# A macaron block on one NeuronCore: the last attention batch moved into the third expert pass, its scatters paced one per pair, and the projection's bias added by GpSimd

## The chip, the cores and the metric

One Trainium2 chip, one of its NeuronCores. The metric is the device time of the whole program in microseconds. Before: median 693.09 us of 3 runs (692.06 to 694.55).

## The reference

x is 16 x 256 x 128 (4096 tokens of 128 channels). Three residual steps, each on the layer-normalised rows:

```python
x = x + 0.5 * moe(layernorm(x))     # 16 experts, top 2
x = x + attention(layernorm(x))     # 16 heads of 8, causal, 256 keys
x = x + 0.5 * moe(layernorm(x))

def moe(xt):
    logits = xt @ Wg.T + bg;  top_vals, top_idx = top_k(logits, 2);  rw = softmax(top_vals)
    gate, up = even, odd columns of xt @ Wgu[e] + bgu[e]
    gated = (clip(up, -7, 7) + 1) * gate * sigmoid(1.702 * gate)     # gate <= 7
    out = sum over the two experts of rw * (gated @ Wd[e] + bd[e])
def attention(x):
    q, k, v = split(x @ W_attn + b_attn);  y = softmax(causal(q k^T / sqrt(8))) v
    return y @ W_proj + b_proj
```

## The kernel before

**Tiles and passes.** The tokens are 32 tiles of 128 rows, in 8 quads of 4 tiles, in 2 sides of 4 quads. Each of the two expert stages routes its tokens: VectorE normalises a quad (`normalise`), TensorE turns it (`transposes`, line 1651) and multiplies by the router's weights (`logits`, 1659), VectorE finds the top two (`top2`), TensorE counts ranks (`ranks`), VectorE makes row numbers (`positions`), and GpSimd scatters each tile's rows twice into `rows_by_expert` in HBM by indirect DMA (`scatter`, line 595; j counts 8 scatters to a quad). A side's rows are then read back, sorted by expert, in 47 tiles, that is 24 pairs. There are four expert passes: 0 and 1 for the first stage, 2 and 3 for the second, one for each side. In the second stage GpSimd gathers the results of pass 2 while pass 3 runs, and those of pass 3 after it (line 530), and VectorE adds them up.

**An expert pass** is a pipeline of slots of one pair, written out by `expert_passes` for each engine. In slot s TensorE turns pair s-1 (`turn_x`, 1740), makes gate and up of pair s-2 (`gate_up`, 1752) and the down product of pair s-4 (`down`, 1764); ScalarE copies xT, takes the sigmoid (866), copies the next weights (854) and issues the store (873); VectorE does `gate` (1292, 1293, 1295; called gate 0, 1, ... by pair) and `evac_y` (1309). SP loads the tiles a turn of eight ahead, in its queue's order: pass 3's loads stand behind all of pass 2's, a table and `s_scat[1]`. After its steps each engine calls a hook, `last_groups` in pass 2, with the slot's number `at`: it holds the routing of the last quads, 6 (`MERGED`) and 7. `s_y` counts finished pairs.

**The attention** between passes 1 and 2 is 64 units of 4 heads of one batch, 4 to a batch, 16 batches, written out in `unit` for each engine; `Steps` says which further steps stand in a unit. TensorE makes scores two units ahead (`late_scores` 1396, `early_scores` 1403), turns the row maxima (1419), makes the transposed scores with mask and maxima (`weights`, 1435 to 1459), and multiplies by the values (`weigh_values`, 1518); ScalarE takes the exponential (715) and copies maxima (709); VectorE takes the row maxima (921, 938). A batch ends with `tokens_first` (1526), `divide`, `channels_first` (1532), `project_out` and `add_attention` (952), which stand in the units of the next batch; for the last batch they stand after all units. `project_out` begins with a product of 3 rows of ones by the bias in three BF16 parts (1537) and adds eight products of the projection (1541) to it in bank 7. The parts are made once by `split_biases` in the first routing and spread by three DMAs of SP. GpSimd's work in the attention (low parts of q and k, adds of expert results at line 553, gathers, scatters of quads 0 to 5) waits for units by `a_max` and `a_pv`. The w_tile buffer of the expert passes lies over pT, the exponentials.

Of the kernel before, what the change touches and what calls it, by code (L numbers as in the profile page):

```python
# [20 lines left out]
ALU = mybir.AluOpType  # L21
# [116 lines left out]
def build_block(nc, x, w_g, g_last, w_gu, up_last, w_d, b_d, attn_last, b_proj, w_attn, w_proj, konst, out):  # L138
    ctx = ExitStack()
    with ctx:  # L140
# [29 lines left out]
        bias_in = sb("bias_in", [1, C])  # L170
        bias_hi = sb("bias_hi", [1, C], BF16)
        bias_mid = sb("bias_mid", [1, C], BF16)
        bias_lo = sb("bias_lo", [1, C], BF16)
        bias3 = sb("bias3", [3, C], BF16)
# [137 lines left out]
        s_bias3 = sem("s_bias3")  # L312
# [115 lines left out]
        def _(sp):  # L428
# [6 lines left out]
            sp.dma_start(bias_in[:, :], b_proj).then_inc(s_bias3, 16)  # L435
# [12 lines left out]

            sp.wait_ge(s_setup, 3)
            for r, part in enumerate((bias_hi, bias_mid, bias_lo)):  # L450
                sp.dma_start(bias3[r:r + 1, :], part[:, :]).then_inc(s_bias3, 16)
# [58 lines left out]
        def _(pool):  # L510
# [38 lines left out]
            def add_result(x, k):  # L549

                mine = xr[:, x * QUAD:(x + 1) * QUAD, :]
                pool.wait_ge(a_half, 2 * x + 1 + k)
                nc.gpsimd.tensor_tensor(mine, mine, yg_of_token[:, :, k, :], ALU.add).then_inc((a_half, a_comb)[k], 1)

# [47 lines left out]
            for f in range(2):  # L602
                if f == 0:
# [31 lines left out]
                    for x in range(1, B // 2):  # L635
# [24 lines left out]
                        if later:  # L660
                            root_of_pair(x + 1)
                        if latest:
# [8 lines left out]
                        else:  # L671
# [4 lines left out]
                            scatter(1, range(26, 37), in_units(u, u, u, u + 1, u + 1, u + 2, u + 2, u + 2, u + 3, u + 3, u + 4))  # L676
                            root(1, MERGED, *GROUPS_2[MERGED])
                            scatter(1, range(37, 48), in_units(u + 5, u + 5) + [(a_pv, u + n) for n in (5, 5, 6, 6, 6, 7, 7, 7, 8)])
                else:
                    root(1, NQ - 1, *GROUPS_2[NQ - 1])  # L680
                    scatter(1, of_quads(6, 8))
# [7 lines left out]
        def attention_scalar(act, normalise_rows, router):  # L689
# [53 lines left out]
            def unit(t, s):  # L743
                t, s = t + s // UNITS, s % UNITS
                steps = Steps(t, s)
                normalise_part(steps, t, s, 0)
                if steps.max_next:
                    evac_max(*after(t, s, 1))
# [9 lines left out]
                exp(t, s)  # L758
# [20 lines left out]
            def units():  # L779
                evac_max(0, 0)  # L780
                attention_units(unit)
                evac_sums(B - 1)
                evac_y_channels(B - 1)

            return first_pair, units

        @block.scalar
        def _(act):
# [28 lines left out]
            for f in range(2):  # L817
                if f == 0:
                    first_pair, units = attention_scalar(act, normalise_rows, router)
# [7 lines left out]
                def last_groups(p, t, k):  # L827
                    if p == SIDES:
                        at = t * DUOS + k
                        if at == 0:  # L830
                            evac_xn(1, MERGED)
                        if at == 4:
# [12 lines left out]
                def copy_weights(p, t, k):  # L845
                    if isinstance(t, int) and (t, k) == (0, 0):
                        act.wait_ge(s_tab, 32 * (p + 1))
                    key = (p, t if isinstance(t, int) else str(t), k // 2)
# [30 lines left out]
        def attention_vector(dve, ch, router, in_tiles):  # L879
# [69 lines left out]
            def add_attention(b):  # L949
                dve.wait_ge(a_proj, b + 2)  # L950
                rows = xs[:, bass.ds((b + 1) * QT, QT), :].rearrange("p n c -> p (n c)")
# [51 lines left out]
            def units():  # L1003
# [4 lines left out]
                divide(B - 1)  # L1008
                add_attention(B - 1)

            return first_pair, units

        @block.vector
        def _(dve):
# [10 lines left out]
            for f in range(2):  # L1025
# [99 lines left out]
                def split_biases():  # L1125
                    dve.wait_ge(s_bias3, 16)
                    ch.mark(nc.vector.tensor_copy(bias_hi[:, :], bias_in[:, :]))
                    ch.wait()
                    ch.mark(nc.vector.tensor_tensor(bias_in[:, :], bias_in[:, :], bias_hi[:, :], ALU.subtract))
                    ch.wait()  # L1130
                    ch.mark(nc.vector.tensor_copy(bias_mid[:, :], bias_in[:, :]))
                    ch.wait()
                    ch.mark(nc.vector.tensor_tensor(bias_in[:, :], bias_in[:, :], bias_mid[:, :], ALU.subtract))
                    ch.wait()
                    nc.vector.tensor_copy(bias_lo[:, :], bias_in[:, :]).then_inc(s_setup, 1)

# [103 lines left out]
                if f == 0:  # L1240
                    first_pair, units = attention_vector(dve, ch, router, in_tiles)
# [694 lines left out]
```

## Time and profile before

| | |
|---|---|
| median of 3 runs | 693.09 us |
| the profiled execution | 689.52 us |
| its span | 687.7 us |
| TensorE, VectorE, ScalarE, GpSimd busy | 70%, 70%, 47%, 50% of the span |
| first routing | to about 78 us |
| passes 0 and 1 | 78 to 196 us, with the first attention steps |
| attention | 200 to 507 us |
| passes 2 and 3 | 511 to 633 us |
| last gathers and adds | to the end |

How to read it: the profile is of one execution. A row of an order of time gives start, duration (both us), engine, line, operation, output <- input and, in brackets, how long the engine stood idle before and what ended that. "PE" is TensorE's products, "DVE" VectorE, "ACT" ScalarE, "POOL" GpSimd. "issue" is a wait that the profile doesn't explain; "remote" one whose releaser it can't name. An engine of which nobody waits costs nothing by being idle.

### The profile page before, as it was taken

What the parts mean: (1) busy time and instruction counts of PE and PEld (TensorE: products, weight loads), DVE (VectorE), ACT (ScalarE), POOL (GpSimd) and SP (SyncE); (2) the same over time, 40 slices, a digit from 0 to 9 for tenths busy, and PEclk for the clock granted to TensorE, in tenths of its full rate; (3) what the DMA queues carried; (4) which work ended last, traced back from release to release, by engine and by line L of the source; (5) the groups of instructions that cost most, each with busy time, mean ns of one, the idle gap of its engine ahead of it and who ended that gap; (6) DMA issues with size and microseconds to landing.
All of it is one profiled execution on the core that took longest, in us unless ns stands there. A gap on an engine that the chain in (4) does not pass through costs nothing.

```text
span 687.7 us, 18833 instructions
## 1 busy us (share of the span) xinstructions
PE 483.6 (70%) x6375; PEld 340.5 (50%) x6375; DVE 482.4 (70%) x2459; ACT 326.6 (47%) x646; POOL 342.4 (50%) x355
## 2 busy tenths in 40 slices
PE   2443488897848898988888888776866789876000
PEld 2433366775625565655555555544445568665000
DVE  6778476887757787889898977766436498666612
ACT  1001376776505656665656564543434378664000
POOL 3757555446356464545454554444524400456774
PEclk9999999998859999999999988999658789999555
DMA  9931255555565362626262523502012335544432
GB/s 268 357 123 47 84 150 155 150 155 136 168 185 181 101 210 70 216 64 215 64 202 75 189 95 126 163 32 63 32 33 85 93 108 152 142 139 127 118 84 62
DMA packets 106294, 89.72 MB, mean 130 GB/s; under 512 B 10977, under 2 KB 98530, under 8 KB 105826
## 3 DMA queue, kind: packets, MB, share of 16 engines
q1 hardware_dynamic: 72130, 59.51, 28.0%
q0 software_dynamic: 8192, 16.79, 8.3%
q10 hardware_dynamic: 25888, 12.34, 6.1%
q8 instruction: 47, 0.77, 0.5%
q14 instruction: 37, 0.30, 0.1%
HBM read 46.93 MB, written 41.68 MB: 129 GB/s over the span
## 4 chain that ended last, share of the span: by engine, by line
PE 44%; DVE 18%; issue 14%; ACT 6%; another core or an unknown queue 6%; POOL 5%; DMA 4%; ACTq 2%; DVEq 0%; SPq 0%; POOLq 0%
PE banks L1752 9%; POOL by_token L530 5%; PE banks L1518 4%; DVE by_token L921 4%; PE banks L1459 3%; PE banks L1403 3%; PE banks L1764 3%; PE banks L1740 2%; PE banks L1659 2%; PE banks L1435 2%; PE banks L1444 2%; PE banks L1439 2%; PE banks L1368 1%; PE banks L1541 1%
## 5 line engine op out<-in xcount | busy, mean ns | idle before, releaser
L921 DVE CUSTOM_DVE_ANT_0 by_token<-banks,konst_sb 128x256 f32<-128x256 f32 (+1 forms) x512 | 151.0, 353 | 41.1 <-PE banks L1403 28.4
L595 POOL DMA_INDIRECT rows_by_expert<-by_token,posi x120 | 118.1, 984 | 109.2 <-DVE maxima L938 39.2
L715 ACT ACTIVATE pT<-banks 128x1536 f32<-128x1536 f32 x64 | 92.9, 1451 | 79.9 <-PE banks L1459 76.8
L1752 PE MATMUL banks<-xT,pT 128*64 128x128 f32 x1504 | 112.1, 289 | 24.8 <-ACT xT L861 10.9
L1752 PEld LDWEIGHTS banks<-xT,pT 128*64 128x64 f32 x1504 | 86.5, 143 | 45.9 <-issue 30.0
L530 POOL DMA_INDIRECT yg<-results_by_tile,tilepos x64 | 62.0, 969 | 77.8 <-DVE maxima L938 38.5
L530 POOL DMA_INDIRECT by_token<-results_by_tile,tilepos x64 | 62.1, 970 | 69.1 <-DMA results_by_tile<-ysb 41.4
L854 ACT ACTIVATE pT<-w_experts 128x384 f32 x188 | 88.2, 516 | 17.5 <-remote 5.5
L1292 DVE SCALAR_TENSOR_TENSOR sig<-banks,sig 128x256 f32<-128x256 f32 x96 | 39.8, 414 | 45.5 <-ACT sig L866 34.0
L1764 PE MATMUL banks<-pT,gT 128*64 128x128 f32 x752 | 62.8, 282 | 3.4 <-DVE ysb L1309 1.6
L866 ACT ACTIVATE sig<-banks 128x256 f32<-128x256 f32 x96 | 36.2, 377 | 51.3 <-PE banks L1752 26.0
L1444 PE MATMUL banks<-q_stack,k_stack 64*128 64x256 bf16 x256 | 58.8, 279 | 0.0
L1518 PE MATMUL banks<-pT,by_token 128*32 128x256 f32 (+1 forms) x1024 | 58.1, 347 | 0.0
L1309 DVE TENSOR_TENSOR ysb<-banks,w_experts 128x128 f32<-128x128 f32 x188 | 45.7, 283 | 15.0 <-PE banks L1764 7.0
L1435 PE MATMUL banks<-mT,select 64*128 64x256 bf16 x256 | 48.6, 279 | 3.3 <-ACT pT L715 3.1
L1764 PEld LDWEIGHTS banks<-pT,gT 128*64 128x64 f32 x752 | 47.7, 142 | 5.3 <-issue 3.9
L709 ACT ACTIVATE mT<-banks 128x256 bf16<-128x256 f32 x64 | 24.5, 383 | 49.4 <-PE banks L1419 41.9
L1403 PE MATMUL banks<-k_stack,q_stack 64*128 64x128 bf16 x256 | 37.0, 226 | 15.0 <-PE banks L1403 5.2
L1740 PE MATMUL banks<-konst_sb,xt 128*128 128x128 f32 x188 | 43.2, 314 | 5.8 <-DVE tabc L1213 3.7
L1459 PE MATMUL banks<-identb,mask_k 64*128 64x128 bf16 x256 | 45.8, 221 | 0.0
L861 ACT ACTIVATE xT<-banks 128x256 f32<-128x256 f32 x96 | 35.5, 370 | 21.5 <-PE banks L1740 13.8
L1295 DVE SCALAR_TENSOR_TENSOR gT<-upc,sig 128x256 f32<-128x256 f32 x96 | 42.3, 440 | 3.3
(165 smaller groups left out, 1019.3 us busy)
## 6 DMA issues: line engine op xcount, KB each, us to landing
xt<-rows_by_expert SPq DMA_DIRECT2D x188, 64.0 KB
results_by_tile<-ysb ACTq DMA_DIRECT2D x92, 128.0 KB
q_stack<-q_by_part SPq DMA_DIRECT2D x8, 1024.0 KB
k_stack<-k_by_part SPq DMA_DIRECT2D x8, 1024.0 KB
q_by_part<-q_parts SPq DMA_DIRECT2D x16, 384.0 KB
k_by_part<-k_parts SPq DMA_DIRECT2D x16, 384.0 KB
x_resident<-in_x SPq DMA_DIRECT2D x8, 256.0 KB, 6.2
w_experts<-in_w_gu SPq DMA_DIRECT2D x1, 2048.0 KB
```

The costliest lines, as they stand in the source:

```text
L530: pool.indirect_dma_start(out=to[:, j, :], out_offset=None, in_=results_dram[q // QSIDE], in_offset=bass.IndirectOffsetOnAxis(ap=tilepos[: ...
L595: pool.indirect_dma_start(out=rows_dram, out_offset=bass.IndirectOffsetOnAxis(ap=posi[:, c:c + 1], axis=0), in_=rows_of(f, q)[:, j // TOPK ...
L715: nc.scalar.activation(pT[:, s % 2, :], banks[:, 3:6, :].rearrange("p a q -> p (a q)"), ACT.Exp, scale=SCALE).then_inc(a_exp, 1)
L854: last = nc.scalar.activation(w_tile[:, 2 * k + i, :], w_all[:, bass.ds(held[key][k % 2 * 2 + i], EW)], ACT.Identity)
L921: nc.vector.tensor_tensor_reduce(masked[:, (3 * g + qt) * P:(3 * g + 2 * qt + 1) * P], of, lag, 1.0, NEG * NEG_BELOW, ALU.add, ALU.max, by ...
L1403: return nc.tensor.matmul(bank[0][:, g * P:(g + 1) * P], q[r, pair, m, o:o + P], k[r, pair, m, o:o + P], start=g == 0, stop=g == GRP - 1)
L1435: nc.tensor.matmul(bank[3 + g % 2][:, g // 2 * T:(g // 2 + 1) * T], select[maxima(g), g // 2, :], mT[maxima(g), s % 2, :], start=g // 2 == ...
L1444: nc.tensor.matmul(bank[3 + g % 2][:, c:c + T], k[r, pair, m, o:o + P], q[r, pair, m, o:o + T], start=False, stop=False)
L1459: return nc.tensor.matmul(to, mask_k[r, half, :], identb[r, r].unsqueeze(1).to_broadcast([HALF, 2, HALF]), start=False, stop=(a, half) == ...
L1518: last = nc.tensor.matmul(bank[6][g * QUARTER:(g + 1) * QUARTER, c + kt * P:c + T], of_head, w, start=j == 0 and kt == 0, stop=j == GRP - ...
L1752: last = nc.tensor.matmul(bank[2 + k % 2][h * HALF:(h + 1) * HALF, at:at + P], w_tile[:, 2 * k + i, which * F + h * HALF:which * F + (h + ...
L1764: last = nc.tensor.matmul(bank[6 + k % 2][h * HALF:(h + 1) * HALF, i * C:(i + 1) * C], gT[:, k, i * P + h * HALF:i * P + (h + 1) * HALF], ...
```

## The change

1. The scatters of quads 6 and 7 get paces: scatter j waits for `s_y` = 2 PAIRS + 1 + j, that is for pair j of pass 2.
2. The end of batch 15 moves from behind the last unit into the hooks of pass 2 (`last_batch`: slot 0, 1, 2), the routing steps of quads 6 and 7 move by up to two slots, and quad 7's statistics go from before the pass into slot 2. ScalarE's first weight copy of pass 2 waits for `a_pv`; TensorE waits for the added rows in slot 4.
3. Unit 0 on TensorE is rewritten: its weights come straight behind its own maxima, ahead of unit 1's early scores; ScalarE takes its exponential first.
4. The bias leaves the projection: it is loaded once to all 128 partitions, and GpSimd adds it to each quad (`add_bias`) once the quad is normalised; `add_attention` waits for `a_biased`. The split of the bias, its three DMAs and the product on line 1537 go.

```diff
-            sp.dma_start(bias_in[:, :], b_proj).then_inc(s_bias3, 16)
+            sp.dma_start(bias_rows[:, :], b_proj.partition_broadcast(P)).then_inc(s_bias, 16)
...
-            sp.wait_ge(s_setup, 3)
-            for r, part in enumerate((bias_hi, bias_mid, bias_lo)):
-                sp.dma_start(bias3[r:r + 1, :], part[:, :]).then_inc(s_bias3, 16)
...
+            def add_bias(x):
+                mine = xr[:, x * QUAD:(x + 1) * QUAD, :]
+                pool.wait_ge(a_xn, x + 1)
+                nc.gpsimd.tensor_tensor(mine, mine, bias_rows[:, :].unsqueeze(1).to_broadcast([P, QUAD, C]), ALU.add).then_inc(a_biased, 1)
...
                         if later:
                             root_of_pair(x + 1)
+                        if x == 1:
+                            pool.wait_ge(s_bias, 16)
+                        add_bias(x - 1)
...
+                            add_bias(x)
                             root(1, MERGED, *GROUPS_2[MERGED])
...
                     root(1, NQ - 1, *GROUPS_2[NQ - 1])
-                    scatter(1, of_quads(6, 8))
+                    scatter(1, of_quads(6, 8), [(s_y, 2 * PAIRS + 1 + j) for j in range(2 * QUAD * TOPK)])
... ScalarE
+                if (t, s) == (0, 0):
+                    exp(t, s)
                 if steps.max_next:
...
-                evac_sums(B - 1)
-                evac_y_channels(B - 1)
+            def last_batch(at):
+                if at == 0:
+                    evac_sums(B - 1)
+                if at == 1:
+                    evac_y_channels(B - 1)
...
                         at = t * DUOS + k
+                        last_batch(at)
                         if at == 0:
                             evac_xn(1, MERGED)
-                        if at == 4:
+                        if at == 5:
                             evac_xn(1, MERGED + 1)
...
+                    if isinstance(t, int) and (p, t, k) == (SIDES, 0, 0):
+                        act.wait_ge(a_pv, B * GRP - 1)
... VectorE
                 dve.wait_ge(a_proj, b + 2)
+                if b >= 0:
+                    dve.wait_ge(a_biased, b // 2 + 1)
...
-                divide(B - 1)
-                add_attention(B - 1)
+            def last_batch(at):
+                if at == 0:
+                    divide(B - 1)
+                if at == 2:
+                    add_attention(B - 1)
...
-                    stats(NQ - 1)
-                    variances(NQ - 1, NQ)
...
+                    last_batch(at)
                     if at == 1:
                         read_logits(MERGED)
                         top2(MERGED)
                     if at == 2:
+                        stats(MERGED + 1)
+                        variances(MERGED + 1, NQ)
+                    if at == 4:
                         normalise(MERGED + 1)
-                    if at == 4:
                         read_ranks(MERGED)
                         positions(MERGED)
-                    if at == 6:
+                    if at == 7:
                         read_logits(MERGED + 1)
                         top2(MERGED + 1)
-                    if at == 8:
+                    if at == 9:
                         read_ranks(MERGED + 1)
                         positions(MERGED + 1)
... (table_counts 9 to 10, table_rest 11 to 12, in_tiles 13 and 15 to 14 and 16) TensorE
                 pe.wait_ge(a_yT, b + 2)
-                nc.tensor.matmul(bank[7][:, 0:QT * C].rearrange("p (n c) -> p n c", c=C), ones[0:3, :],
-                                 bias3[0:3, :].unsqueeze(1).to_broadcast([3, QT, C]), start=True, stop=False)
...
-                                                w_out[:, :], start=False, stop=i == QT - 1)
+                                                w_out[:, :], start=i == 0, stop=i == QT - 1)
...
+                if n == 0:
+                    project(0, steps.q)
+                    late_scores(0, 2)
+                    max_T(0, 1)
+                    early_scores(0, 2)
+                    return
...
                 max_T(0, 0)
+                weights(0, 0, None)
                 early_scores(0, 1)
...
-                tokens_first(B - 1)
-                channels_first(B - 1)
-                project_out(B - 1)
+            def last_batch(at):
+                if at == 0:
+                    tokens_first(B - 1)
+                if at == 1:
+                    channels_first(B - 1)
+                if at == 2:
+                    project_out(B - 1)
+                if at == 4:
+                    pe.wait_ge(a_x2, B + 1)
...
                     if at == 0:
                         transposes(MERGED)
+                    if at == 1:
                         logits(MERGED)
+                    last_batch(at)
                     if at == 3:
                         ranks(MERGED)
-                    if at == 4:
+                    if at == 5:
                         transposes(MERGED + 1)
-                    if at == 5:
+                    if at == 6:
                         logits(MERGED + 1)
-                    if at == 7:
+                    if at == 8:
                         ranks(MERGED + 1)
                         counts(3)
-                    if at == 10:
+                    if at == 11:
                         sums(3)
```

## Rows read from the trace of the kernel before

**Rows 1.** The chain of waits after pass 3 (start us, us, what): first and last gather

```profile
631.82 0.95 POOL by_token L530
...
677.31 0.95 POOL by_token L530
```

**Rows 2.** Windows, line 1740 alone: start:end, length, busy and operations of PE and PEld

```profile
581.40:588.70 7.30, 1.75 (x8) 0.81 (x8) 1.00 0.60 164
78.30:126.80 48.50, 10.54 (x46) 5.04 (x46) 1.00 0.48 141
141.00:154.60 13.60, 3.03 (x14) 1.37 (x14) 1.00 0.63 169
590.60:625.20 34.60, 6.12 (x28) 2.82 (x28) 1.00 0.50 137
```

**Rows 3.** Windows, whole core: length, busy of PE, PEld, DVE, ACT, POOL, clock, DMA, GB/s

```profile
581.40:588.70 7.30, 7.30 (x108) 5.97 (x104) 6.46 (x21) 6.50 (x18) 0.00 (x0) 1.00 0.60 164
78.30:126.80 48.50, 42.83 (x558) 34.01 (x558) 34.98 (x106) 33.96 (x88) 27.24 (x27) 1.00 0.48 141
141.00:154.60 13.60, 12.88 (x184) 10.41 (x182) 10.69 (x33) 10.45 (x28) 7.55 (x8) 1.00 0.63 169
590.60:625.20 34.60, 27.14 (x367) 21.38 (x364) 21.48 (x68) 21.57 (x56) 20.86 (x22) 1.00 0.50 137
516.80:576.70 59.90, 46.73 (x565) 36.72 (x564) 42.25 (x152) 33.15 (x85) 15.54 (x16) 0.89 0.35 102
503.70:510.80 7.10, 5.03 (x24) 3.55 (x24) 2.70 (x13) 1.92 (x4) 1.03 (x1) 0.50 0.04 12
```

**Rows 4.** Order of time, GpSimd: first and last scatter of quad 6

```profile
521.54 1.03 POOL L595 DMA_INDIRECT rows_by_expert<-by_token,posi  x1 [11.01 <-DVE posi L1123]
...
530.51 0.97 POOL L595 DMA_INDIRECT rows_by_expert<-by_token,posi  x1 [0.30 <-issue]
```

**Rows 5.** Order of time, TensorE and ScalarE inside that burst

```profile
523.61 1.09 PE L1752 MATMUL banks<-xT,pT 128*64 128x128 f32 x16
...
533.12 0.38 ACT L866 ACTIVATE sig<-banks 128x256 f32<-128x256 f32 x1 [4.60 <-remote]
```

**Rows 6.** Order of time, end of the attention, TensorE and ScalarE

```profile
496.90 1.51 PE L1518 MATMUL banks<-pT,by_token 128*32 128x256 f32 x16
...
502.01 0.60 ACT L722 ACTIVATE ysum<-banks 128x512 f32<-128x512 f32 x1 [5.80 <-remote]
...
502.75 1.08 PE L1526 MATMUL banks<-konst_sb,ysum 128*128 128x128 f32 x4 [4.34 <-ACT ysum L722]
...
504.74 0.69 PE L1532 MATMUL banks<-konst_sb,yn 128*128 128x128 f32 x2 [0.91 <-DVE yn L946]
...
505.91 0.39 PE L1537 MATMUL banks<-bias,ones 3*128 3x256 bf16 x1 [0.48 <-ACT yT L726]
...
507.28 1.12 PE L1651 MATMUL banks<-konst_sb,by_token 128*128 128x128 f32 x4
...
509.08 1.89 PE L1659 MATMUL banks<-wg,xnT 128*128 128x16 f32 x8 [0.69 <-ACT xnT L800]
```

**Rows 7.** Order of time, VectorE, the normalise of one quad

```profile
488.57 1.20 DVE L1050 TENSOR_SCALAR by_token<-x_resident,mv,rstd 128x127 f32<-128x127 f32 x4
```

**Rows 8.** The chain of waits inside the attention: one bias product

```profile
322.41 0.21 PE banks L1537
```

**Rows 9.** Lines 553 and 1295 (ns min/median/max), and the GpSimd multiply beside the longest 1295

```profile
L553 POOL TENSOR_TENSOR x_resident<-x_resident,yg x16: 1273/1290/1437, 158.8 to 387.9; 128x512 f32<-128x512 f32 x16
...
L1295 DVE SCALAR_TENSOR_TENSOR gT<-upc,sig x96: 291/425/1730, 83.5 to 632.7; 128x256 f32<-128x256 f32 x92, 128x128 f32<-128x128 f32 x4
...
185.24 1.91 POOL L546 TENSOR_TENSOR yg<-yg,wts 128x1024 f32<-128x1024 f32 x1 [3.05 <-DMA yg<-results_by_tile,tilepos]
```

**Rows 10.** Order of time, TensorE, start of unit 1's weights

```profile
212.11 0.27 PE L1435 MATMUL banks<-mT,select 64*128 64x256 bf16 x1 [0.79 <-ACT pT L715]
```

**Rows 11.** Order of time, VectorE in the first routing, first operation of the bias split

```profile
24.86 0.21 DVE L1127 CAST bias_hi<-bias_in 1x128 bf16<-1x128 f32 x1
```

More of the change, by code:

```diff
@@ L168, in build_block @@
         zeros = sb("zeros", [P, C])
[L170 to L174, printed above, removed]
+        bias_rows = sb("bias_rows", [P, C])
         by_token = sb("by_token", [P, NT * TOPK * C])
@@ L311, in build_block @@
         s_x = [sem(f"s_x{i}") for i in range(NQ)]
-        s_bias3 = sem("s_bias3")
+        s_bias = sem("s_bias")
+        a_biased = sem("a_biased")
         s_setup = sem("s_setup")
@@ L757, in unit @@
                     evac_y_channels(steps.project)
-                exp(t, s)
+                if (t, s) != (0, 0):
+                    exp(t, s)
                 if steps.x is not None:
@@ L781, in units @@
                 attention_units(unit)
-                evac_sums(B - 1)
-                evac_y_channels(B - 1)
-            return first_pair, units
+            def last_batch(at):
[3 more added lines that the diff above has]
+                    evac_y_channels(B - 1)
+            return first_pair, units, last_batch
         @block.scalar
@@ L818, in _ @@
                 if f == 0:
-                    first_pair, units = attention_scalar(act, normalise_rows, router)
+                    first_pair, units, last_batch = attention_scalar(act, normalise_rows, router)
                 else:
@@ L1007, in units @@
                 attention_units(unit)
-                divide(B - 1)
-                add_attention(B - 1)
-            return first_pair, units
+            def last_batch(at):
[3 more added lines that the diff above has]
+                    add_attention(B - 1)
+            return first_pair, units, last_batch
         @block.vector
@@ L1123, in positions @@
                     nc.vector.tensor_copy(posi[:, cs], posf[:, cs]).then_inc(s_pos, 1)
[L1125 to L1135, printed above, removed]
                 def router(t, s, reading):
@@ L1240, in _ @@
                 if f == 0:
-                    first_pair, units = attention_vector(dve, ch, router, in_tiles)
+                    first_pair, units, last_batch = attention_vector(dve, ch, router, in_tiles)
                     def spread_of(group):
@@ L1259, in _ @@
                             normalise(1)
-                        if q == 1:
-                            split_biases()
                         if q == 2:
@@ L1320, in last_groups @@
                     if at == 2:
+                        stats(MERGED + 1)
+                        variances(MERGED + 1, NQ)
+                    if at == 4:
                         normalise(MERGED + 1)
-                    if at == 4:
                         read_ranks(MERGED)
                         positions(MERGED)
-                    if at == 6:
+                    if at == 7:
                         read_logits(MERGED + 1)
                         top2(MERGED + 1)
-                    if at == 8:
+                    if at == 9:
                         read_ranks(MERGED + 1)
                         positions(MERGED + 1)
-                    if at == 9:
+                    if at == 10:
                         table_counts(3)
-                    if at == 11:
+                    if at == 12:
                         table_rest(3)
-                    if at == 13:
+                    if at == 14:
                         in_tiles(2)
-                    if at == 15:
+                    if at == 16:
                         in_tiles(3)
@@ L1550, in first_pair @@
                     pe.wait_ge(s_asetup, 6)
-                    pe.wait_ge(s_bias3, 64)
                     rows_T(0, 4)
@@ L1633, in units @@
                 bank7_free(TURNS_A - 1, UNITS - 1)
-                tokens_first(B - 1)
-                channels_first(B - 1)
-                project_out(B - 1)
-            return first_pair, units
+            def last_batch(at):
[7 more added lines that the diff above has]
+                    pe.wait_ge(a_x2, B + 1)
+            return first_pair, units, last_batch
         @block.tensor
@@ L1695, in _ @@
                 if f == 0:
-                    first_pair, units = attention_tensor(pe, small_products, transposes)
+                    first_pair, units, last_batch = attention_tensor(pe, small_products, transposes)
                 else:
```

## The prediction

> **What bounds the kernel now.** I read the chain of waits first, then the granted-clock windows, then the order of time around each place that the diff touches. The chain ends in a run of 37 GpSimd gathers, one each 1.26 us, which starts when pass 3 ends [rows 1]. The change leaves this tail alone, so what brings the end of pass 3 forward comes off the time one to one.
>
> The second view compares stretches of the expert passes by pairs of tiles (two transposes of line 1740 per pair). Without indirect DMAs 4 pairs take 7.3 us, 1.83 each; with 8 gathers beside 7 pairs 13.6 us, 1.94 each; in pass 0, with a scatter paced to each pair, 23 pairs take 48.5 us, 2.11 each; in pass 3, with 22 gathers to 14 pairs, 34.6 us, 2.47 each [rows 2, 3]. Pass 2 is the odd one: 59.9 us from gate 1 to gate 22, 21 pairs at 2.85, though VectorE is busy in only 42.25 us of them [rows 3]. The reader is to see that 17.6 us of idle sit there.
>
> The third view says where. Quads 6 and 7 are scattered in two bursts of eight, one DMA each 1.27 us without a pause, the first from 521.54 to 531.48 [rows 4]. Inside it TensorE ends a gate/up product at 524.70 (523.61 + 1.09), and ScalarE, which needs nothing but that, starts on it at 533.12 [rows 5]. The profile finds no late releaser ("remote"), so I read: while indirect DMAs follow each other without a pause, the engines' signals to each other arrive late. The same shows at the end of the attention, where quad 5's scatters run: the last value product ends at 498.41, ScalarE copies its sums at 502.01 [rows 6].
>
> **The change part by part.** The profiled execution took 689.52 us (span 687.7 and 1.8 around it), 0.5% below the median of 693.09; the sum is made against the first and its difference applied to the second.
>
> *Scatters one per pair.* Each of the 16 waits for one more finished pair, so the bursts end. The stretch without them: VectorE's 42.25 plus one normalise (1.2, [rows 7]) that now falls into it, 43.5, if VectorE is never idle; 21 pairs at 1.83, 38.4, plus VectorE's router work (42.25 less 21 times the 1.61 that it is busy per undisturbed pair, plus 1.2: 9.5) 47.9, if none of it overlaps. I take 46.5, nearer the second, since this work comes in lumps of 1 to 3 us, and the engines hand on pair by pair. Then the scatters' own toll. A gather per pair costs (13.6 - 12.8)/8 = 0.1 us, a scatter per pair (48.5 - 42.1)/26 = 0.25 (27 operations, one of them a memset), gathers at three to two pairs (34.6 - 25.6)/22 = 0.41 [rows 2, 3]. I take 0.3: pass 0 is the same operation at the same pace, a little more because VectorE is fuller here; 16 x 0.3 = 4.8. 46.5 + 4.8 - 59.9 = **-8.6** (43.5 + 1.6 and 47.9 + 6.6: -14.8 to -5.4). Who waits for the last scatter: SP, before it loads pass 3's tiles. It goes out when pair 15 is done, in slot 19 or 20; the tiles are needed in slot 25, 10 us later, cover enough for its landing, the table and the load. Without that cover it costs the difference, which I put at nothing.
>
> *The last batch inside pass 2.* Before, TensorE waits 0.91, 0.48 and 0.69 us between its steps after 502.75, and its transposes of quad 6 (1.12) stand behind the projection though nothing holds them [rows 6]. Now these fall into the 4.34 us wait for the sums, and the three waits are covered by the first tiles, whose loads landed long ago. [...] TensorE's new wait for the added rows in slot 4 has two slots of cover; ScalarE's, for the next to last value product, ends before ScalarE gets there. The 3.6 us before the sums stay, for quad 5's scatters stay.
>
> *Bias product out of the projection.* 15 in the attention, each on the chain with 0.21 us [rows 8]: 3.15, **-3.0** (0 to 3.2; 0 if VectorE ends each unit last).
>
> *Bias by GpSimd.* Eight adds of 128x512, as line 553's at 1.29 us [rows 9], each put where GpSimd next waits for a unit and needed three units later, so VectorE's new wait is covered. Behind each a gather is queued, in a gap of about that length. [...] VectorE has few such instructions in an attention unit, and short ones: **+0.4** (0 to 8 x 1.3 = 10.4). [...]
>
> *First unit's weights ahead.* They come straight behind unit 0's maxima, and a projection and the next two units' scores move behind them. The wait of 0.79 us for the first exponential [rows 10] goes. But unit 1's maxima are late by what unit 0's weights take at the low clock; I have no row for these alone and estimate 1.8 us, so unit 1's weights start at 212.11 - 0.79 + 1.8 = 213.1: **+1.0** (-0.8 to +2).
>
> *Setup.* Five small VectorE operations, some 1.4 us from 24.86 on [rows 11], and three tiny DMAs of SP go; one load of 64 KB comes. GpSimd's scatters set the pace there too: **-0.7** (-1.5 to +0.3).
>
> Sum: -8.6 - 3.0 - 3.0 + 0.4 + 1.0 - 0.7 = -13.9, so 675.6 for the profiled execution and **679.2 us** for the median.
>
> **Rivals.** *A, the toll is larger.* A lone scatter may hold signals back for much of a pair, and VectorE's gate waits for its own signal inside each pair. It decides at (59.9 - 46.5 + 5.3)/16 = 1.17 us per scatter: above it the kernel is slower than before. At 1.5 us it is 5.3 us slower, 698. For it: the bursts cost (59.9 - 46.5)/16 = 0.84 each, and a paced scatter meets a new pair each time. Against it: 0.1 to 0.41 everywhere else in this trace. 6%.
>
> *B, the bursts are innocent.* The stalls come from the router's own chain (top two, ranks) and only coincide with the scatters, or the change's pacing doesn't thin them. Then pass 2 keeps its 59.9 and the rest gives -5.3: 687.8. Against it: ScalarE's wait of 8.4 us (524.70 to 533.12) has no router step in it. [...] 12%.
>
> *C, pass 2 becomes clean.* The tolls hide, VectorE is never idle and the clock stays up: -14.8 - 5.5 - 2.3 = -22.6, 670.5. For it: the clock's mean in the stretch is 0.89, and 1.00 in every stretch without a stall [rows 3]. 17%.
>
> [...] Adds at 0.6 us each and the first unit at +2 make +5.4 against the sum: 684.6. 7%.
>
> **How the numbers follow.** My own case, 673 to 685, has 58%. A measurement of this kernel tells 0.3%, 2.1 us, from no change. Slower than that: A, 6%. Within it: the upper edge of B and the lower of A, 7%. Faster: 87%. The range for 8 in 10 takes in C and the middle of B: 670 to 688.
>
> **What would show it.** In pass 2 GpSimd's scatters some 2 us apart, no ScalarE wait above 2.5 us, gate 1 to gate 22 in about 51 us. At the pass's head the first gate/up product within 6 us of the sums' transposes, where now the logits alone start 6.3 us after them. No line 1537 product; GpSimd adds of 1.3 us and no VectorE instruction stretched beside them. Wrong, if ScalarE still waits 4 us and more with the scatters apart (B), if pairs with a scatter take over 2.8 us (A), or if pass 3 starts with a wait for its tiles.

## The result, and the profile after

The changed kernel takes **680.8 us** (median of 4 runs, 679.8 to 682.6) where the kernel before took 692.6 beside it (median of 4, 691.9 to 694.6): ratio 0.984, 95% interval 0.9815 to 0.9865, 11.8 us less. The prediction was 679.2, in the range of 670 to 688. The two profiled executions stand 6.9 us apart (682.6 and 689.5), since the profiled one of after is the slowest of its four and the one of before lies below all of its four. So the stretches below are compared with those of further executions, and the sum with the runs.

First the page of the changed kernel: span, busy time, the clock by slices and the chain's shares.

```profile
span 680.8 us, 18817 instructions
PE 481.3 (71%) x6358; PEld 339.7 (50%) x6358; DVE 487.2 (72%) x2454; ACT 327.5 (48%) x646; POOL 352.5 (52%) x363
...
PEclk9999999899865998999999996997788899999555
...
PE 40%; issue 16%; DVE 15%; SPq 7%; DMA 6%; POOL 6%; ACT 4%; another core or an unknown queue 4%; ACTq 2%; DVEq 0%; POOLq 0%
```

Busy time hardly moved: idle time went. GpSimd's busy time rose by the 8 adds (10.2 us), VectorE's by 4.8 us, of which 4.0 lie beside adds, as the part on the prediction shows. Pass 2 next, in the columns of [rows 3], from gate 1 to gate 22:

```profile
518.60:569.50 50.90, 41.20 (x556) 33.51 (x553) 42.75 (x158) 33.08 (x83) 16.76 (x17) 0.97 0.41 118
```

50.9 us against 59.9 [rows 3] for the same 21 pairs and the same work of VectorE, at a clock of 0.97 in place of 0.89. The scatters (instruction, count, ns min/median/max, first and last start) are no longer 1.27 us apart [rows 4]:

```profile
L593 POOL DMA_INDIRECT rows_by_expert<-by_token,posi x13: 962/966/1033, 505.3 to 540.9; - x13
L593 POOL DMA_INDIRECT rows_by_expert<-q_rest,posi x8: 962/965/1187, 545.0 to 560.7; - x8
```

The last 8 of the first line are quad 6's, from 524.0 (the five before them are quad 5's); the second line is quad 7. The head of pass 2, in order of time, answers to [rows 6]:

```profile
505.90 0.88 PE L1523 MATMUL banks<-pT,by_token 128*32 128x256 f32 x16
...
508.58 0.60 ACT L724 ACTIVATE ysum<-banks 128x512 f32<-128x512 f32 x1 [0.16 <-remote]
...
509.23 0.99 PE L1531 MATMUL banks<-konst_sb,ysum 128*128 128x128 f32 x4 [1.01 <-ACT ysum L724]
...
510.02 0.63 PE L1758 MATMUL banks<-konst_sb,xt 128*128 128x128 f32 x2
...
513.03 1.98 PE L1770 MATMUL banks<-xT,pT 128*64 128x128 f32 x16
```

From the transposes of the sums to the first gate/up product it is now 3.8 us (509.23 to 513.03). Before it was 9.2: 502.75 [rows 6] to 511.99, where the trace of before has its first line 1752 of the pass. The scatters of quad 5 still run beside it.

What did not come is seen at the first unit. In order of time, TensorE, ScalarE, VectorE and GpSimd:

```profile
207.96 0.95 POOL L523 DMA_INDIRECT yg<-results_by_tile,tilepos  x1 [0.30 <-issue]
210.49 1.45 ACT L717 ACTIVATE pT<-banks 128x1536 f32<-128x1536 f32 x1 [4.30 <-remote]
...
210.56 0.39 PE L1408 MATMUL banks<-k_stack,q_stack 64*128 64x128 bf16 x2 [2.65 <-remote]
...
210.99 0.29 DVE L933 CUSTOM_DVE_ANT_0 by_token<-banks,konst_sb 128x128 f32<-128x128 f32 x1 [5.61 <-PE banks L1408]
```

The weights of unit 0 are done by 207.7, yet the exponential starts at 210.49, 2.8 us later, and VectorE starts on the early scores only at 210.99. The last of 8 gathers back to back (199.1 to 208.9) stands in that time. Still, the exponential comes 16.4 us after pass 1's last gate, before it came 18.9 us after it; what is lost comes behind it. The exponential of unit 1 starts at 219.9, before at 213.5. Between the two exponentials TensorE now has almost no idle time, at the low clock (the first line is after, the second before):

```profile
210.50:219.90 9.40, 8.81 (x54) 3.86 (x58) 6.81 (x37) 3.23 (x6) 4.90 (x4) 0.53 0.04 14
```

```profile
210.50:213.50 3.00, 2.21 (x36) 1.31 (x38) 2.59 (x15) 2.23 (x5) 2.38 (x3) 1.00 0.00 0
```

So the 9.4 us are for the most part the work that the new order puts there (early scores, two projections of 2.07 us, maxima, unit 1's weights), at a granted clock of 0.53 in place of 1.00.

The stretches of both profiled kernels, in us (an exponential is named by its unit):

| stretch | before | after | difference |
|---|---|---|---|
| start to the first tile's transposes | 78.3 | 73.1 | -5.2 |
| from there to pass 1's last gate | 113.3 | 121.0 | +7.7 |
| that gate to exponential 1 | 21.9 | 25.8 | +3.9 |
| exponential 1 to 50 | 215.2 | 215.7 | +0.5 |
| exponential 50 to 63 | 66.0 | 68.6 | +2.6 |
| exponential 63 to pass 2's gate 0 | 20.0 | 11.5 | -8.5 |
| gate 0 to gate 1 | 2.2 | 3.0 | +0.8 |
| gate 1 to gate 22 | 59.9 | 50.9 | -9.0 |
| gate 22 to pass 3's last gate | 55.4 | 55.8 | +0.4 |

### The profile page after: what moved, and what is told of

Read it like the earlier page. It is cut to its first block, busy times and chain, and to the rows that moved or that the text cites. A ratio compares the mean times of both kernels' runs of the same rounds, so it can differ in the third digit from the quotient of the medians.

```text
span 680.8 us, 18817 instructions
## 1 busy us (share of the span) xinstructions
PE 481.3 (71%) x6358; PEld 339.7 (50%) x6358; DVE 487.2 (72%) x2454; ACT 327.5 (48%) x646; POOL 352.5 (52%) x363
## 4 chain that ended last, share of the span: by engine, by line
PE 40%; issue 16%; DVE 15%; SPq 7%; DMA 6%; POOL 6%; ACT 4%; another core or an unknown queue 4%; ACTq 2%; DVEq 0%; POOLq 0%
PE banks L1770 8%; POOL by_token L523 5%; DVE by_token L933 4%; PE banks L1523 4%; PE banks L1782 3%; PE banks L1408 3%; PE banks L1758 3%; DMA k_stack<-k_by_part 2%; PE banks L1373 2%; PE banks L1464 2%; PE banks L1440 2%; SPq L439 2%; PE banks L1449 2%; PE banks L1444 2%
## 5 line engine op out<-in xcount | busy, mean ns | idle before, releaser
L1770 PE MATMUL banks<-xT,pT 128*64 128x128 f32 x1504 | 110.1, 289 | 23.0 <-ACT xT L873 11.1
L1523 PE MATMUL banks<-pT,by_token 128*32 128x256 f32 (+1 forms) x1024 | 59.7, 354 | 0.0
L1311 DVE TENSOR_TENSOR ysb<-banks,w_experts 128x128 f32<-128x128 f32 x188 | 45.8, 283 | 16.1 <-PE banks L1782 10.2
L1464 PE MATMUL banks<-identb,mask_k 64*128 64x128 bf16 x256 | 46.5, 225 | 0.0
```

The source lines that it names most:

```text
L1464: return nc.tensor.matmul(to, mask_k[r, half, :], identb[r, r].unsqueeze(1).to_broadcast([HALF, 2, HALF]), start=False, stop=(a, half) == ...
L1523: last = nc.tensor.matmul(bank[6][g * QUARTER:(g + 1) * QUARTER, c + kt * P:c + T], of_head, w, start=j == 0 and kt == 0, stop=j == GRP - ...
L1770: last = nc.tensor.matmul(bank[2 + k % 2][h * HALF:(h + 1) * HALF, at:at + P], w_tile[:, 2 * k + i, which * F + h * HALF:which * F + (h + ...
```

## Experiments

The twelve runs fall into six groups, each on one chip and beside its own runs of the kernel before. All ratios are to that kernel in the same group, with 95% intervals; where two ratios of different groups are compared, both groups are of the same level (the word is explained below). I tested these causes: bursts hold signals back (theory), or they are innocent (rival B); and, for each other part, my term against nothing.

**The paces taken away, the old first unit, the old bias, the paces alone.**

```diff
- scatter(1, of_quads(6, 8), [(s_y, 2 * PAIRS + 1 + j) for j in range(2 * QUAD * TOPK)])
+ scatter(1, of_quads(6, 8))
```

The second undoes the hunks of `exp` in ScalarE's `unit`, of `n == 0` in TensorE's `unit` and of `weights(0, 0, None)`; the third undoes every hunk on the bias; the fourth adds only the line with the paces to the kernel before.

> The changed kernel without the scatters' paces in pass 2; all else as changed. My theory (scatters back to back hold the engines' signals back): the 16 scatters go 1.27 us apart in two bursts, gate 1 to gate 22 goes from 50.9 us back to about 59, ScalarE waits 4 us or more inside each burst, and the time is 7 to 9 us longer, about 689. Rival (bursts innocent; pass 2 gained because the router's steps were moved and the last batch joined it): gate 1 to gate 22 stays within 2 us of 50.9 and the time within 2 us of the changed kernel's 680.8.

> The changed kernel with the order of before in the attention's first unit. Theory: the new order put the early scores of unit 0 and 1 into the burst of 8 gathers (199.1 to 208.9), where their signal to VectorE came 5.6 us late; so the old order takes the second exponential from 219.9 back to about 213.5 and the time is 5.5 to 6.5 us shorter, about 675. Rival (the burst of gathers meets whatever stands there, and the old order loses as much elsewhere): the second exponential stays after 217 and the time changes by less than 2 us.

> The changed kernel with the bias product back in the projection, no GpSimd adds, the small setup operations of before. By my prediction's terms: 2.6 us longer by the attention (15 products at 0.21 less 0.4) and 0.7 in the setup, 684. Rival (VectorE or a wait ends each unit, so the product was hidden; from unit 1 to unit 63 the changed kernel gained nothing on the one before): 0 to 1 us longer. [...]

> The kernel before with the scatters of pass 2 one per pair, and nothing else of the change. Theory: gate 1 to gate 22 goes from 59.9 to about 51 us and the time is 8 to 9 us shorter, about 684. Rival (the paces help only where the last batch and the router's steps are moved with them, since quad 6's positions come late): the gain is under 4 us.

Nobody expected what came: here the kernel before took 611.3 us, not 693. The four took 610.3 (0.9982, 0.9957 to 1.0006), 608.9 (0.9957, 0.993 to 0.9983), 609.7 (0.9977, 0.9945 to 1.001) and 611.5 (1.0007, 0.9977 to 1.0036). The whole change by itself, in a group that gave 611.8 for the kernel before:

> The changed kernel itself, unaltered, beside the kernel before. On the chip of the first four experiments the kernel before took 611.3 us where the chip of the prediction gave 693, and the signals arrive at once there (in nine of ten cases within 0.02 us), also beside indirect DMAs. Theory (the change's gain in pass 2 exists only where indirect DMAs hold signals back): if this run falls on such a chip, the change gives 0 to 2 us, about 610, and gate 1 to gate 22 takes the same 48 to 50 us with and without paces; if it falls on a chip like the first, 11 to 13 us, about 681. Rival (the first four experiments each lost something that the whole change has, so the change is worth its 11 us anywhere): 1.5 to 2% shorter on either chip.

It took 610.0, ratio 0.9957 (0.9914 to 0.9999). So its 1.6% are not worth the same everywhere.

> The kernel before itself, unaltered, for its profile where the chip is another. Theory (late signals are the chip's, and the bursts cost only through them): where signals arrive at once, gate 1 to gate 22 takes 48 to 51 us in two bursts, against 59.9 on the first chip, pass 0 takes 1.9 us a pair against 2.1, and the head of pass 2 still takes 14 to 15 us. Rival (the bursts cost VectorE or TensorE something else too, a port or the memory): gate 1 to gate 22 stays at 55 us or more. If the chip is like the first, 59 to 60 us and 692 in all.

This one came out at 691.3 and 688.3. Two levels, then, and one level per group: all runs within a group agree. The chip does not decide it: the one with number 2 on record gave 688 us in this group and 612.9 in the last one below. I call the level of 611 us the prompt one and that of 692 us the delayed one; the prediction and its traces are of the delayed one.

The traces tell the levels apart by how soon an engine starts once what it waits for is done. Take ScalarE where it waits for TensorE's products alone, some 270 places in each profile. In the seven profiles of the prompt level it never starts more than 0.5 us late. Late means here: after both the product and ScalarE's own work before are done. In the seven of the delayed level it starts more than 1 us late at 21 to 28 of them, up to 6.0 us, and nearly always (all but 3 of the 170) an indirect DMA of GpSimd runs in that time. VectorE's first step of a gate, which waits for ScalarE's sigmoid, is late at neither level (at most 0.41 us in 96 places of each profile), beside indirect DMAs too, and TensorE's gate/up products, which wait for ScalarE's copies, start at most 0.90 us late at the delayed level (96 places of each profile). So what is seen to come late is what TensorE hands on, and not every engine's signal, as the theory had it. Whether it is the signal that is late or the product itself, no trace shows: the ends of matmuls are modelled.

Two more differences. DMA packets take the same time at both levels (GpSimd's 0.11 us in the mean), so a busier memory is not seen. But the traces of the delayed level hold 8,500 to 8,700 records of semaphore updates, those of the prompt one 13,300, for the same program: a third of the records is missing. The lateness of these records is therefore no measure. In the kernel before, the next record of the sigmoid's semaphore after its end at 525.44 comes 8 us later, and the gate that waits for it starts at 525.48. Whether the recording itself takes part in the delayed level is an open rival that no run here tests.

The run without paces has both. Its windows from gate 1 to gate 22, first at the prompt level, then at the delayed one:

> The changed kernel without the paces once more, in the hope of a chip of the first kind (kernel before at 688 to 693 us). Theory: there gate 1 to gate 22 is 8 to 9 us longer than the changed kernel's 50.9, signals arrive up to 8 us late in the two bursts, and the ratio to the kernel before is 0.995 to 0.998 in place of 0.984. Rival: ratio 0.984 as with the paces. On a chip of the second kind (611 us) both say 0.998 again.

```profile
458.35:506.89 48.54, 38.69 (x540) 31.49 (x539) 42.83 (x158) 32.59 (x80) 16.72 (x17) 1.00 0.43 124
```

```profile
519.19:584.52 65.33, 47.49 (x540) 36.39 (x539) 42.93 (x158) 32.13 (x80) 16.84 (x17) 0.84 0.32 91
```

One program, the same two bursts of eight, the same work of VectorE: 48.5 us or 65.3. The gate/up products inside the first burst, in order of time, prompt level:

```profile
463.21 1.09 PE L1770 MATMUL banks<-xT,pT 128*64 128x128 f32 x16
465.94 1.09 PE L1770 MATMUL banks<-xT,pT 128*64 128x128 f32 x16
467.76 1.09 PE L1770 MATMUL banks<-xT,pT 128*64 128x128 f32 x16
```

and delayed level, with the scatters of the burst and ScalarE's wait behind it:

```profile
526.78 1.09 PE L1770 MATMUL banks<-xT,pT 128*64 128x128 f32 x16
...
530.17 0.62 PE L1770 MATMUL banks<-xT,pT 128*64 128x128 f32 x7 [0.62 <-issue]
531.08 0.27 PE L1770 MATMUL banks<-xT,pT 128*64 128x128 f32 x1 [0.29 <-issue]
531.79 0.42 PE L1770 MATMUL banks<-xT,pT 128*64 128x128 f32 x3 [0.45 <-issue]
532.50 0.37 PE L1770 MATMUL banks<-xT,pT 128*64 128x128 f32 x1 [0.29 <-issue]
533.21 0.71 PE L1770 MATMUL banks<-xT,pT 128*64 128x128 f32 x4 [0.34 <-issue]
```

```profile
524.54 1.03 POOL L593 DMA_INDIRECT rows_by_expert<-by_token,posi  x1 [4.14 <-DVE posi L1141]
...
533.77 0.97 POOL L593 DMA_INDIRECT rows_by_expert<-by_token,posi  x1 [0.30 <-issue]
```

```profile
536.09 0.38 ACT L878 ACTIVATE sig<-banks 128x256 f32<-128x256 f32 x1 [6.02 <-remote]
```

There is more in this than a late start of the waiting engine. A product of 16 matmuls takes 1.09 us; here one is torn into pieces over 3.75 us (530.17 to 533.92), though nothing inside it waits for another engine ("issue"). The sigmoid at 536.09 does not belong to this product but to the one before it, of 526.78, which was done at 527.87: ScalarE starts on it 8.2 us after its end, 6.02 of them idle, and on the torn one at 537.46. The time was 698.5 us, ratio **1.0091** (1.007 to 1.0112): *without the paces the change makes the kernel slower*. At this level the theory holds in direction (bursts cost, pacing gains), and its size was too small: 17 us against the changed kernel's 0.984, not 7 to 9. At the prompt level rival B's picture is the right one. The rest of the change is thus worth nothing with the paces (0.984 against 0.9843 for the paces alone, below) and costs 6 us without them; why its bursts cost more than those of the kernel before (65.3 us in the stretch against 59.9) is not shown.

**The old first unit, delayed level.**

> The changed kernel with the old order of the first unit once more, for a chip of the first kind. Theory: the second exponential comes 3.0 us after the first instead of 9.4 and the time is 5.5 to 6.5 us shorter than the changed kernel's: ratio to before 0.975 to 0.977. Rival (part of the gap lies in the low clock and the projection that now stand between the two exponentials, as on the second kind of chip, where the old order gave 1 to 3 us): ratio 0.980 to 0.983.

679.3 us, 0.9821 (0.9785 to 0.9857). The interval takes in the changed kernel's 0.984 as well as half of the gain that the theory gave it, so the runs don't decide. The profiles give a size: from pass 1's last gate to exponential 1 it is 22.6 us here and 20.3 to 22.5 in the other kernels with the order of before, against 25.8 and 26.1 in the two with the new one. Some 4 us of that stretch (3.2 to 5.8) are the new order; the theory's 5.5 to 6.5 were too many. And its cause was the wrong one. At the prompt level, where nothing arrives late, the new order still puts 8.6 to 9.9 us between the exponentials 0 and 1 (9.4 and 9.5 at the delayed level), the old one 2.9 to 3.0 (3.0 to 4.0). There unit 0's exponential starts 0.05 us after its weights, and the stretch from the last gate is 21.9 to 25.0 us with the new order and 20.1 to 21.8 with the old one. The changed kernel at the prompt level, from exponential 0 to 1:

```profile
186.40:195.00 8.60, 7.55 (x56) 3.59 (x58) 6.34 (x37) 3.19 (x5) 6.05 (x6) 0.71 0.08 22
```

TensorE is busy in 7.55 of the 8.60 us, here too.

**The paces alone, and more of them, delayed level.** The second has the old first unit, and this:

```diff
- scatter(1, range(37, 48), in_units(u + 5, u + 5) + [(a_pv, u + n) for n in (5, 5, 6, 6, 6, 7, 7, 7, 8)])
+ scatter(1, range(37, 39), in_units(u + 5, u + 5))
...
- scatter(1, of_quads(6, 8), [(s_y, 2 * PAIRS + 1 + j) for j in range(2 * QUAD * TOPK)])
+ scatter(1, range(39, 64), [(s_y, 2 * PAIRS + 1 + j * 2 // 3) for j in range(25)])
```

> The kernel before with the scatters of pass 2 one per pair and nothing else, for a chip of the first kind (kernel before at 688 to 693 us). Theory (the paces are what gains, and stand alone): gate 1 to gate 22 takes 50 to 52 us against 59.9 and the time is 8 to 9 us shorter, ratio 0.986 to 0.989. Rival, from the run without paces, which was 5.9 us slower than the kernel before: the paces mostly repair what the last batch inside the pass costs beside bursts, and alone give less, 3 to 6 us, ratio 0.991 to 0.996. On a chip of the second kind, 1.00 again.

> The changed kernel with the old order of the first unit, and with the last 9 scatters of quad 5 moved out of the end of the attention into pass 2, where 25 scatters now go at three to two pairs. Theory (a scatter costs 0.8 us and more in a burst and 0.3 to 0.45 when spread): on the first kind of chip the end of the attention and the head of pass 2 get 5 to 8 us shorter, pass 2 gets 3 to 6 us longer, and the time is 1 to 4 us below that of the old order alone (679.3), 675 to 678. Rival (three to two pairs in a pass where VectorE is full is a burst again): pass 2 loses more than is gained, 680 and more. On the second kind of chip (611 us) both say within 1.5 us of 609.

The paces alone: 680.5 us, ratio 0.9843 (0.9812 to 0.9874). That is, at the delayed level, **the whole gain of the change from one line**. The windows of gate 1 to gate 22, paces alone, then spread:

```profile
514.94:565.05 50.11, 41.80 (x564) 34.14 (x565) 41.71 (x153) 33.15 (x84) 15.57 (x16) 0.97 0.41 120
```

```profile
508.06:560.66 52.60, 41.08 (x543) 33.13 (x542) 42.49 (x158) 31.08 (x81) 25.32 (x26) 0.97 0.42 124
```

The spread one: **670.9 us**, 0.9691 (0.9651 to 0.973), 10 us below the changed kernel and under what I expected. Nine more scatters in pass 2 cost it 52.6 - 50.2 = 2.4 us against the same kernel without the move (50.2), 0.27 each. They save 1.6 us between exponentials 50 and 63 (67.9 to 66.3) and 3.3 us at the head (11.7 to 8.4). The profiled spans differ by 6.2 (677.8 and 671.6), the runs by 1.3%, 9 us; the two ratios are of different groups, and the stretches that the edit touches make up 2.5 us (1.6 + 3.3 - 2.4). Most of the rest of the 6.2 lies where nothing was edited, so how much of the 9 us is the spreading stays open; no second run at this level was made.

**The last batch, and the bias, by difference.** First, the kernel before with the paces and the last batch inside pass 2 (the changed kernel with the old first unit and the old bias); second, the spread one with the old bias.

> The kernel before with the paces and with the last batch inside pass 2; no GpSimd adds (bias product in the projection, setup of before), old order of the first unit. For a chip of the first kind. Against the paces alone (ratio 0.984) it shows the last batch, against the changed kernel with the old first unit (0.982) the bias change. Theory P (the last batch is worth 3 us by my prediction, the profiles' head of pass 2 says 8, less 1 to 2 given back in the pass; and the bias change loses 3 us before the attention, where gate 47 stands at 191.6 to 192.5 without it and at 194.1 to 196.0 with it): 675 to 677, ratio 0.975 to 0.979. Rival (the last batch gives its gain back at the end of the attention, and the bias change is worth nothing either way): 679 to 681, ratio 0.981 to 0.984. My prediction's bias term (3.0 gained, 0.4 and 0.7 around it) would give 682, ratio 0.986.

> The run with 25 scatters spread over pass 2, with the bias product back in the projection and no GpSimd adds. Theory P: 3 to 4 us below the 670.9 of that run, ratio 0.963 to 0.966. Rival (bias change worth nothing): ratio 0.968 to 0.971. Spread alone, against the other run of this pair: 6 to 9 us shorter, as it was from 0.982 to 0.969; if that was luck of the chip, under 3 us.

The group fell on the prompt level (612.9 us for the kernel before), which my numbers were not made for: 608.5 and 608.2 us, both 0.9918 (0.9882 to 0.9955; 0.9885 to 0.995). Spreading is worth nothing there (0.0), and the paces were worth nothing (1.0007), but the last batch is: 0.9918 against 1.0007, 5.4 us. For the delayed level, what the last batch and the bias give one by one stays open; together they take the ratio from 0.9843 to 0.9821, 1.5 us give or take 3.3, which is not clear of nothing.

## Why the prediction was right, and where it was not

The direction, the likeliest case and its main term held: -11.8 us in the runs against -13.9. Of the six terms only the first came out near its value; the other five were off, and the total came so close by luck, since they cancelled.

*Scatters one per pair, -8.6.* Right as a stretch: 51.3 forecast, 50.9 after, 50.1 with the paces alone. Its two parts were off against each other. The bare stretch at the prompt level, even with bursts, is 48.5, not 46.5; what is left for 16 paced scatters is 2.4 us, 0.15 each by this estimate, not 0.3. The span gained 10.6 us with the paces alone (687.7 to 677.1), where the stretch gained 9.8. Rivals A and B fall by these rows: ScalarE's longest wait in the stretch is 3.15 us (above the 2.5 that I named, below the 4 of B), and the toll is 0.15, not A's 1.17. At the prompt level B comes true all the same (gate 1 to gate 22: 48.5 us with bursts, 49.1 paced); at the delayed one it does not (65.3 and 50.9). My own reading, that the engines' signals to each other arrive late, was too wide: those of ScalarE to VectorE do not, what TensorE hands on does.

*Last batch, -3.0 (0.3 to 5.5).* Undersized. The head fell by 8.5 us in the two profiles and by 6.9 at the prompt level (14.4 to 7.5), of which 0.8 to 2.2 come back inside the pass, and 5.4 show in the prompt level's runs. No run shows my 3.0. It was added up from the waits between the projection's steps, the transposes of quad 6 and the bias product (2.1, 1.1 and 0.3 us), less 0.5 for waits of the new order. The step that failed: it left the products on the path, at the granted clock of 0.50. In fact the first tile's products moved past them, 5.4 us from transposes to gate/up. And the wait for the sums, which I held fixed, is no constant: the kernel before's head was 20.0 us in one execution and 16.6 in another.

*Bias product out, -3.0.* This term failed. I counted all 15 products of 0.21 us as on the chain; 12 of them are, and one of those is shown [rows 8]. But from exponential 1 to 50 the two kernels take 215.2 and 215.7 us. At the prompt level two pairs of kernels differ by the bias change alone, the two of a pair from different groups. In one it moves the ratio from 0.9977 to 0.9957 (1.2 us gained), in the other from 0.9918 to 0.9957 (2.4 us lost), each within the intervals, so nothing that can be measured. The bound of 0 that I gave fits best; the chain's share was not what removing it gains.

*Bias by GpSimd, +0.4.* The adds take 1.27 us each. The 0.4 was my estimate, and so was its upper end of 8 x 1.3, from one gate product with two inputs in SBUF that took 1.73 us and not 0.43 beside a GpSimd multiply [rows 9]; no run shows either of them. The profile after shows 4.0 us in its place, and I had said that no VectorE instruction would be stretched. Lines (ns min/median/max, first and last start) of the add and of three VectorE instructions of the changed kernel:

```profile
L551 POOL TENSOR_TENSOR x_resident<-x_resident,bias_rows x8: 1272/1274/1283, 231.4 to 492.7; 128x512 f32<-128x512 f32 x8
```

```profile
L950 DVE TENSOR_TENSOR maxima<-maxima x64: 176/178/525, 203.8 to 496.4; 128x8 bf16<-128x8 f32 x64
L1197 DVE TENSOR_SCALAR ntile<-cntr x4: 215/216/2001, 42.7 to 542.0; 16x128 bf16<-16x128 f32 x4
L1060 DVE TENSOR_SCALAR less<-mv x8: 169/169/1359, 267.5 to 518.5; 128x4 f32<-128x4 f32 x8
```

The maximum of line 1060 stands beside the add at 492.74 in all 7 profiles of kernels with the adds (1.36 us), and in none of the 7 without them (0.17). Line 1197's (0.22 before in the median, 2.00) stands beside the add at 434.71 and on the chain, in three of the 7. That makes 1.8 + 1.2 us, and four times 0.24 for line 950 beside other adds: 4.0 stretched in all, over my 0.4. Exponential 50 to 63 is 1 to 2.6 us longer in the delayed kernels with adds (67.9 to 68.6; without them 66.0, 66.0 and 66.8), save in the one whose nine scatters were moved out of that stretch (66.3). I had looked only for instructions with two inputs in SBUF; those of lines 1060 and 1197, 1.36 and 2.00 us where 0.17 and 0.22 are the median, have one. By what they are held up is not shown.

*First unit, +1.0 (-0.8 to +2).* About 4 us in the stretch; the sign was right, the size outside my bounds. The step that failed: I named what moves behind unit 0's weights (a projection and the scores) and priced the weights alone, at 1.8 us. TensorE's work between the exponentials 0 and 1 is 8.8 us at a clock of 0.53, where before it was 2.2 us at 1.00, and the gap is there at the prompt level too (8.6 to 9.9 us). The burst of gathers adds the 2.8 us by which exponential 0 starts after its weights, at the delayed level only; I had not priced these either.

*Setup, -0.7.* Not seen in the stretches. The start of the first tile varies between 73.0 and 79.0 us with and without the change, and pass 1's last gate stands at 191.6, 192.5 and 191.7 in the kernels with the old setup, at 194.1 to 196.0 in those with the new one. That 3 us loss at the delayed level is not explained; at the prompt level it is not there (173.1 to 173.6 with the new setup, 173.1 to 177.4 with the old one).

The errors largely cancel: against the forecast the last batch gave 5 us more; the first unit gave 3 less, exponential 1 to 63, where the bias terms were to show, some 6 less (+3.1 against -2.6), and the time up to pass 1's last gate some 3 less (+2.5 against -0.7). Together that is the 7 us by which the profiled executions fall short of the sum (-6.9 against -13.9), while the runs fall short by 2.1 alone. The net of everything but the paces is 0.9843 to 0.984, nothing.

## What to carry to other kernels

Spread indirect DMAs over the work beside them, one per step, rather than letting a queue of them run free: at the delayed level that one line is worth all 11 us of this change, and the run with nine more of them moved was faster still (670.9 us, one run, 2.5 us of it seen in the stretches touched), while at the prompt level it costs nothing (ratio 1.0007). An instruction's time on the chain is not what removing it gains: here 12 products of 0.21 us on the chain were worth nothing that could be measured. When an order is changed, price everything that moves between two steps, at the clock that is granted there (here 8.8 us of TensorE at 0.53 where I had 1.8). A kernel is compared with runs of the same group alone. Before an elementwise instruction goes to GpSimd, list which VectorE instructions will stand beside it, the small ones too: here they came to 4.0 us beside eight adds.

## What was not expected of the hardware

The same program takes 611 or 692 us, 13%, by the group, on one chip too. At the delayed level ScalarE stands idle for up to 6.0 us though the product that it waits for is done, nearly always beside indirect DMAs, and a run of matmuls without any wait is torn apart by "issue" gaps; VectorE's starts behind ScalarE stay within 0.41 us. GpSimd's own time per indirect DMA is the same (0.98 us each at both levels), and TensorE's granted clock is the lower where it stalls more (0.84 in the stretch of 65.3 us, 1.00 in that of 48.5). What puts a group on one level or the other no run here shows, nor whether the recording, which loses a third of its semaphore records at the delayed level, has a part in it. For VectorE, one small TENSOR_SCALAR (169 ns alone) took 1,359 ns beside a GpSimd add of 1,280.
